# Local attention after a convolution block: P's blocks moved by SP's DMA queue, and another order of the work of images 1 to 3

## The chip, the cores and the metric

The kernel runs on one core of a Trainium2 chip. The metric is the device time of one execution in microseconds, as the median of several runs. Engines are named as in the profile: PE (TensorE, matmul; PEld is its weight load), DVE (VectorE), ACT (ScalarE), POOL (GpSimd), SP (SyncE, which here only issues DMAs).

## The reference, cut to what matters

There are 16 images of 32 x 32 pixels with 128 channels, float32.

```python
perceived = depthwise_conv3x3(x, w_perc) + b_perc        # 128 -> 384 channels
hid = gelu(w_up1 @ perceived + b_up1)                    # 256 channels
h = x + w_up2 @ hid + b_up2                              # 128 channels
q, k, v = split(h @ w_qkv.T + b_qkv)
scores = [(q * shifted(k, dy, dx)).sum(-1) / sqrt(128) for dy, dx in the 3 x 3 window]   # zero padded
w = softmax(scores)                                      # over the 9 positions
out = h + sum_i w[i] * shifted(v, dy_i, dx_i)
```

## The kernel before

Depthwise filters and `w_up1` are folded into one 3 x 3 convolution from 128 to 256 channels. It is computed with a transform along the row (four pixels, six products `M_ORDER`), so that an image needs, for each half of the 256 channels, six **units** of nine products each (L469: three row taps, each as high x high, low x high, high x low, since an operand is split into a rounded "high" part and the "low" rest). Units 0 to 5 are half 0, units 6 to 11 half 1. For every image n the engines do:

- DVE `transform_ab` and `transform` and POOL `differences` and `sums_ab` form the transformed pixels `t`; ACT `high_t` rounds them to `thi`, DVE `low_t` subtracts to `tlo`.
- PE units write PSUM banks. ACT `take_m13` copies one bank, DVE `combine` (ps_sb, ru_sb), `combine_y` (four lines, L1043 to L1049) and `finish_y` (L1057) make `y`. ACT `gelu` (L716) makes `hid`, ACT `high_hid` (L726) rounds it, POOL `low_hid` (L1345) subtracts.
- PE `up(n)` (L524) is the second product, for image n - 1: six products that need the first channel half's high and low parts, four that need the rounding of the second half (`hhi_done`), two that need its low part (`hlo_done`). DVE `sum_h` adds x to give h. ACT `high_h` and DVE `low_h` split h, PE `project_q_parts` (L560 to L563), ACT `take_q`, PE `project_v` (L568) and `score` (L577) follow. A score is a tile of 128 queries against 96 near keys.
- DVE `softmax_front` adds keys for the zero padding and takes the row maxima; ACT takes the exponentials (L795, eight tiles, `exp`); DVE `sums` the reciprocals; POOL `normalise` (L1352); DVE `turn_p` (L1111) transposes P by 32 x 32 blocks into `ptc`.
- The 32-row blocks of `ptc` have to stand at other partitions and columns in `pt`, where PE `values` (L594) reads them. `place_p` on ACT does this with twelve copies (L781, one for each of four rows and three neighbouring rows, 32 partitions x 7 or 8 tiles x 32 numbers). DVE `add_h` adds h to the values, and SP stores the result.

`body(n)` of each engine handles the convolution of image n, the attention scores of image n - 1, the placing of P of image n - 2, and values of image n - 3. Below, numbers in brackets are the arguments in the code, so `up(2)` is in body 2 and multiplies image 1's hid; `gelu(1,1)`, `high_hid(1,1)` and `low_hid(1,1)` are the second half of image 1. "Image n" as a stretch of time is body n. Orders are written out by hand; semaphores count each step. Bodies 0 to 2 have orders of their own, 3, 14 and 15 and the loop in between (bodies 4 to 13) share one. Each engine works strictly in its written order.

The loads and stores are issued by SP in this order: planes of image n + 2, rows of image n + 1 (after `sum_h`), stores. An exponential needs another ACT table than gelu; `prime_gelu` behind the exponentials brings gelu's back.

Of the kernel before, what the change touches and what calls it, by code (L numbers as in the profile page):

```python
# [83 lines left out]
def build(nc, x_planes, x_rows, w_perc, b_perc, w1_c, b_up1, w2_c, b_up2, wqk_c, wv_c, b_qkv, ident_bf_c,  # L84
          mask_c, zero_c, out):
    with ExitStack() as ctx:
# [168 lines left out]
        pt_done = sem("pt_done")  # L255
        pt_dve_done = sem("pt_dve_done")
# [17 lines left out]
        PLACED = TR * 3  # L274
        LATE = ((B - 3, 0), (B - 3, 1), (B - 2, 0), (B - 2, 1), (B - 1, 0))
# [81 lines left out]
        def _(sp):  # L357
# [44 lines left out]

            def body(n, par, conv, attn, store, more):
                if conv and (not isinstance(n, int) or n + 2 < B):

                    sp.wait_ge(ab_done, n * 2 + 2)
                    sp.wait_ge(fcge_done, n * 3 + 3)
                    load_planes(n + 2, par)
                if attn and (not isinstance(n, int) or n + 1 < B):

                    sp.wait_ge(h_done, n * 2)
                    load_rows(n + 1, 1 - par)
                if store and from_image(n, 3):
                    store_out(n)
# [6 lines left out]
        def _(pe):  # L421
# [18 lines left out]
            def small_weights():  # L440
                pe.wait_ge(weights_in, 16 * N_W)
                wq, wk = wqk_in[:, 0, :], wqk_in[:, 1, :]
                pe.matmul(work[:, 2, P:2 * P], wq, wk, start=True, stop=True)
                pe.matmul(work[:, 2, 2 * P:2 * P + 1], wq, bqk[:, 1:2], start=True, stop=True)
                pe.matmul(work[:, 2, 2 * P + 1:2 * P + 2], wk, bqk[:, 0:1], start=True, stop=True)
                pe.wait_ge(biases_in, 48)
                for g in range(2):
                    for m in range(3):
                        last = pe.matmul(work[:, 2, g:g + 1], w1T[:, m, g * P:(g + 1) * P], bp[:, m:m + 1],
                                         start=(m == 0), stop=(m == 2))  # L450
                last.then_inc(b1_ready, 1)
                pe.wait_ge(bq_wide_done, 1)
                pe.matmul(work[:, 2, 2 * P + 2:2 * P + 3], bq_wide[:, :], bqk[:, 1:2], start=True,
                          stop=True).then_inc(wt_ready, 1)
                for _ in range(4):
                    last = pe.matmul(m_ps[:, 2, S:CH], w1T[:, 0, 0:P], w1T[:, 0, 0:S], start=True, stop=True)
                last.then_inc(warm_done, 1)
# [124 lines left out]
            def values(n, hp, g):  # L582

                if not isinstance(n, int) or n < B:

                    pe.wait_ge(v_done, n * 3 - 6)
                    pe.wait_ge(pt_done, n * PLACED - 2 * PLACED)
                    pe.wait_ge(rmax_done, n * 8 + (4 * g - 12))
# [10 lines left out]
            def last_attention():  # L599
# [8 lines left out]
                pe.wait_ge(pt_done, (n - 2) * PLACED)  # L608
# [24 lines left out]
                pe.wait_ge(pt_done, (n - 2) * PLACED + 6)  # L633
# [6 lines left out]
                for g, fillers in enumerate((5, 3)):  # L640
                    for _ in range(fillers):
                        pe.matmul(s_ps[:, 0, 0:S], whi[:, M_ORDER[0], 0, 0:P], thi[:, 0, 0, :], start=True, stop=True)
                    pe.wait_ge(pt_done, (n - 2) * PLACED + 12 + 6 * g)
                    pe.wait_ge(pt_dve_done, 12 + 6 * g)
                    values(n + 2, 1, g)
# [46 lines left out]
        def _(act):  # L692
# [90 lines left out]
            def place_p(n, par, rows):  # L783

                if isinstance(n, int) and n == 2:
                    act.wait_ge(zeroed, 5)
                act.wait_ge(ptc_done, n * 2 - 2)
                if from_image(n, 4):
                    act.wait_ge(o_ready, n * 2 - 6)
                for row in rows:  # L790
                    place(par, row)
# [53 lines left out]
            def body(n, par, conv, attn, store, more):  # L845
# [8 lines left out]
                if is_image(n, 1):  # L854
# [11 lines left out]
                    gelu(1, 1)  # L866
                    for i in range(T):
                        exp(1, i)
                    prime_gelu()
                    return  # L870
                if is_image(n, 2):
                    high_hid(1, 1)
                    take_m13(2, 0)
                    place_p(2, 0, (0, 1, 2))
                    for c in range(NCH):
                        high_h(2, 1, c)
                    place_p(2, 0, (3,))
# [9 lines left out]
                    return  # L887
                if attn:
                    gelu(n - 1, 1)
# [4 lines left out]
                if store:  # L894
                    place_p(n, par, (0, 1, 2, 3))
# [23 lines left out]
        def _(dve):  # L919
# [59 lines left out]
            for k, i in enumerate(TAPS):  # L979

                for m in (1, 2):
# [9 lines left out]
                    if k == 1 and m == 1:  # L991
                        transform_ab(0, 0)
# [109 lines left out]
            def turn_p(n, g):  # L1102

                dve.wait_ge(pn_done, n * 2 + (g - 1))
                if is_last(n):
                    dve.wait_ge(pt_done, (n - 2) * PLACED + 6)
                    dve.wait_ge(pt_dve_done, 6)
                elif from_image(n, 2):
                    dve.wait_ge(pt_done, n * PLACED - PLACED)
# [102 lines left out]
            def body(n, par, conv, attn, store, more):  # L1212
# [12 lines left out]
                if is_image(n, 1):  # L1225
# [12 lines left out]
                    for g in range(2):  # L1238
                        sums(1, g)
                        turn_p(1, g)  # L1240
                    return
                if is_image(n, 2):
                    transform_ab(3, 1)
                    combine(2, 0)
                    sum_h(2, 0)
                    low_h(2, 1)
# [6 lines left out]
                    sums(2, 0)  # L1253
                    combine_y(2, 1)
                    finish_y(2, 1)
                    turn_p(2, 0)
                    sums(2, 1)
                    turn_p(2, 1)
                    return
# [44 lines left out]
        def _(pool):  # L1304
# [67 lines left out]
            def body(n, par, conv, attn, store, more):  # L1372
# [10 lines left out]
                else:  # L1383
# [58 lines left out]
```

## Time and profile before

| what | us |
|---|---|
| median of 3 runs (lowest, highest) | 404.14 (403.94, 404.82) |
| the profiled execution | 405.43 |
| its span, first to last instruction | 403.1 |
| PE busy in the span | 386.1 (96%) |
| DVE busy | 340.5 (84%) |
| ACT busy | 320.6 (80%) |
| POOL busy | 177.4 (44%) |

The busy time of an engine is the union of its instructions; issuing a DMA and waiting are not counted. PE's granted clock is given as a share of full speed (1.00 is 2.4 GHz). "Idle before, releaser" names what ended an engine's gap. A `x2` in the rows in order of time means that neighbouring instructions of one form were merged.

### The profile page before, as it was taken

How to read it: one execution, taken by the hardware profiler on the slowest of the kernel's cores; microseconds unless marked ns; L12 is line 12 of the kernel's file. 1: busy time of each engine (PE TensorE's matmuls, PEld its weight loads, DVE VectorE, ACT ScalarE, POOL GpSimd, SP SyncE). 2: the span in 40 equal slices, each digit the busy share in tenths (PEclk: the TensorE clock that was granted, in tenths of full speed). 3: DMA queues.
4: the chain of work that ended last, by engine and by line, in shares of the span. 5: the costliest groups of instructions: out<-in, count | busy, mean ns of one | idle time of the engine just before them, and what ended most of it. 6: DMA issues, size and time to landing. Idle time of an engine off the chain costs nothing.

```text
span 403.1 us, 10500 instructions
## 1 busy us (share of the span) xinstructions
PE 386.1 (96%) x3674; PEld 362.9 (90%) x3674; DVE 340.5 (84%) x922; ACT 320.6 (80%) x710; POOL 177.4 (44%) x156
## 2 busy tenths in 40 slices
PE   6999975999999999999999999999999999999994
PEld 5999964998999999999999999999999999999874
DVE  5999975798898888888898888889888888886785
ACT  7635568789797997979798897979799797978873
POOL 6785164362626354351636354351636345032110
PEclk9999996999999999999999999999999999999999
DMA  7420300204013050504013050503104030301003
GB/s 232 167 65 2 120 0 18 101 2 146 28 55 116 2 172 1 169 0 131 38 34 135 0 169 0 169 0 104 65 12 157 0 104 2 104 2 54 3 37 120
DMA packets 11513, 28.57 MB, mean 71 GB/s; under 512 B 2400, under 2 KB 3296, under 8 KB 11488
## 3 DMA queue, kind: packets, MB, share of 16 engines
q1 hardware_dynamic: 11200, 28.21, 20.6%
q8 instruction: 14, 0.23, 0.2%
q14 instruction: 11, 0.09, 0.1%
q10 hardware_dynamic: 288, 0.05, 0.1%
HBM read 19.86 MB, written 8.39 MB: 70 GB/s over the span
## 4 chain that ended last, share of the span: by engine, by line
PE 73%; DVE 4%; issue 1%; POOL 0%; DVEq 0%; ACT 0%
PE m_ps L469 39%; PE s_ps L594 8%; PE work L524 8%; PE work L568 6%; PE s_ps L577 5%; PE s_ps L563 2%; PE s_ps L560 1%; PE s_ps L561 1%; PE work L594 1%; DVE t L946 1%; PE work L547 0%; DVE o_sb L1120 0%; PE m_ps L606 0%; DVE ptc L1111 0%; DVE pt L1126 0%
## 5 line engine op out<-in xcount | busy, mean ns | idle before, releaser
L469 PE MATMUL m_ps<-thi,whi 128*128 128x256 f32 x558 | 159.7, 286 | 0.7 <-DVE ru_sb L1034 0.4
L469 PE MATMUL m_ps<-thi,wlo 128*128 128x256 f32 x558 | 156.2, 280 | 0.0
L469 PE MATMUL m_ps<-tlo,whi 128*128 128x256 f32 x558 | 155.0, 278 | 0.0
L469 PEld LDWEIGHTS m_ps<-thi,whi 128*128 128x128 f32 x558 | 105.7, 189 | 4.0 <-issue 1.0
L469 PEld LDWEIGHTS m_ps<-tlo,whi 128*128 128x128 f32 x558 | 106.5, 191 | 0.7
L469 PEld LDWEIGHTS m_ps<-thi,wlo 128*128 128x128 f32 x558 | 105.6, 189 | 0.0
L1345 POOL TENSOR_TENSOR hid_lo<-hid,hid_hi 128x1024 fp32r<-128x1024 f32 x30 | 72.4, 2412 | 24.9 <-ACT hid_hi L726 20.4
L781 ACT COPY pt<-ptc 32x256 f32<-32x256 f32 (+3 forms) x186 | 73.0, 393 | 5.5 <-DVE ptc L1111 1.0
L1322 POOL TENSOR_TENSOR fc<-xp 128x512 f32<-128x512 f32 x16 | 21.6, 1347 | 110.1 <-DVE tlo L953 106.7
L716 ACT ACTIVATE hid<-y,b1eff 128x1024 f32<-128x1024 f32 x31 | 35.6, 1150 | 36.5 <-DVE y L1057 26.7
L795 ACT ACTIVATE p_sb<-p_sb,negmax 128x101 f32<-128x101 f32 x128 | 46.8, 369 | 7.0 <-DVE negmax L1092 7.0
L1352 POOL TENSOR_TENSOR p_sb<-p_sb,rsum 128x384 f32<-128x384 f32 x32 | 27.8, 868 | 42.0 <-DVE rsum L1100 41.9
L594 PE MATMUL s_ps<-pt,v_sb 128*128 128x192 f32 (+2 forms) x260 | 39.0, 305 | 0.0
L594 PEld LDWEIGHTS s_ps<-pt,v_sb 128*128 128x128 f32 x260 | 37.3, 190 | 0.0
L1033 DVE TENSOR_TENSOR ps_sb<-m,m_ps 128x512 f32<-128x512 f32 x32 | 21.7, 678 | 15.2 <-ACT m L706 15.2
L726 ACT CAST hid_hi<-hid 128x1024 fp32r<-128x1024 f32 x30 | 31.5, 1051 | 0.1
L953 DVE TENSOR_TENSOR tlo<-t,thi 128x1024 fp32r<-128x1024 f32 (+1 forms) x30 | 28.1, 978 | 2.7 <-ACT thi L700 2.7
L568 PEld LDWEIGHTS work<-wvT,h_around 128*128 128x128 f32 x240 | 29.1, 192 | 1.2
L700 ACT CAST thi<-t 128x1024 fp32r<-128x1024 f32 (+1 forms) x32 | 25.1, 832 | 5.8 <-DVE t L946 5.6
L568 PE MATMUL work<-wvT,h_around 128*128 128x129 f32 x240 | 29.2, 275 | 0.0
L524 PE MATMUL work<-hid_hi,w2hi 128*128 128x512 f32 x60 | 23.8, 397 | 4.0 <-ACT hid_hi L726 3.7
L1330 POOL TENSOR_TENSOR t<-ab 128x256 f32<-128x256 f32 x16 | 11.8, 738 | 35.8 <-DVE ab L938 35.8
(157 smaller groups left out, 787.5 us busy)
## 6 DMA issues: line engine op xcount, KB each, us to landing
xp<-x_planes SPq DMA_DIRECT2D x16, 640.0 KB, 5.2
xr<-x_rows SPq DMA_DIRECT2D x16, 512.0 KB, 4.0
out<-o_sb SPq DMA_DIRECT2D x28, 256.0 KB, 4.1
out<-y SPq DMA_DIRECT2D x3, 256.0 KB, 2.4
w1T<-w SPq DMA_DIRECT2D x1, 384.0 KB, 3.0
out<-y SPq DMA_DIRECT2D x2, 128.0 KB, 2.5
w2T<-w SPq DMA_DIRECT2D x1, 128.0 KB, 4.4
wqk_in<-w_qk SPq DMA_DIRECT2D x1, 128.0 KB, 4.3
```

The source lines that it names most:

```text
L469: last = pe.matmul(bank[:, col + first:col + end], a[:, j, dy, half * P:(half + 1) * P], c[:, par, T_PLACE[j], first + by:end + by], start ...
L524: return pe.matmul(up_bank(n, c), w[:, half * C:(half + 1) * C], h[:, half, c * CH:(c + 1) * CH], **kw)
L568: last = pe.matmul(v_bank(n, part)[:, u * VT:(u + 1) * VT], h_of(n - 1, hp)[:, W + i * P:W + (i + 1) * P], wvT[:, :], start=True, stop=True)
L594: last = pe.matmul(o_bank(n, g)[:, (first - g * half) * W:(end - g * half) * W], v_of(n - 3, hp)[:, i, :], pt[:, hp, i, (first - above) * ...
L700: nc.scalar.copy(thi[:, par, part, :], t[:, part, :]).then_inc(thi_done, 1)
L716: nc.scalar.activation(hid[:, half, :].rearrange("p (r k s) -> p k r s", k=K4, s=WIN), y[:, half, :, :].rearrange("p k (r s) -> p k r s", ...
L726: nc.scalar.copy(hid_hi[:, half, :], hid[:, half, :]).then_inc(hhi_done, 1)
L781: nc.scalar.copy(pt[to_rows, hp, to_there, to_cols], ptc[rows, there, cols]).then_inc(pt_done, 1)
L795: nc.scalar.activation(p_sb[:, i, 0:KEYS], p_sb[:, i, 0:KEYS], ACT.Exp, bias=negmax[:, i:i + 1], scale=-1.0, accum_out=p_sum[:, i:i + 1]). ...
L953: nc.vector.tensor_tensor(tlo[:, par, part, :], t[:, part, :], thi[:, par, part, :].bitcast(F32), ALU.subtract).then_inc(tlo_done, 1)
L1345: nc.gpsimd.tensor_tensor(hid_lo[:, half, :], hid[:, half, :], hid_hi[:, half, :].bitcast(F32), ALU.subtract).then_inc(hlo_done, 1)
L1352: nc.gpsimd.tensor_tensor(p_sb[:, tiles, 0:NEAR], p_sb[:, tiles, 0:NEAR], rsum[:, tiles].unsqueeze(2).to_broadcast([P, 4, NEAR]), ALU.mult ...
```

## The change

P's blocks are no longer copied by ACT in bodies 2 to 15, but moved by twelve DMA transfers of SP's queue, issued after the planes' load and ahead of the rows' load. They count on a semaphore of their own, `pt_moved` (16 for each transfer, `MOVED` is 192 an image), on which PE's `values` and DVE's `turn_p` now wait. The last image keeps copies on ACT and DVE.

In body 1 ACT rounds the second half of image 1's hid and takes the next bank ahead of the exponentials; POOL forms image 3's differences before the low halves, waits until DVE has made y, does both low halves in a row and only then normalises. DVE's order changes in bodies 1 to 3, and body 3 gets an order of its own on ACT and DVE. In the front, there are three warm-up products instead of four, and `transform_ab(0, 0)` stands one line later.

```diff
@@ SP's program
+            def move_p(n, par):
+                if isinstance(n, int) and n == 2:
+                    sp.wait_ge(zeroed, 5)
+                sp.wait_ge(ptc_done, n * 2 - 2)
+                for row in range(TR):
+                    for rows, there, cols, to_rows, to_there, to_cols in p_blocks(row):
+                        sp.dma_start(pt[to_rows, par, to_there, to_cols], ptc[rows, there, cols]).then_inc(pt_moved, 16)
             def body(n, par, conv, attn, store, more):
                 if conv and (not isinstance(n, int) or n + 2 < B):
                     sp.wait_ge(ab_done, n * 2 + 2)
                     sp.wait_ge(fcge_done, n * 3 + 3)
                     load_planes(n + 2, par)
+                if store:
+                    move_p(n, par)
                 if attn and (not isinstance(n, int) or n + 1 < B):
                     sp.wait_ge(h_done, n * 2)
@@ PE: small_weights, values, last_attention
-                for _ in range(4):
+                for _ in range(3):
                     last = pe.matmul(m_ps[:, 2, S:CH], w1T[:, 0, 0:P], w1T[:, 0, 0:S], start=True, stop=True)
...
-                    pe.wait_ge(pt_done, n * PLACED - 2 * PLACED)
+                    pe.wait_ge(pt_moved, n * MOVED - 2 * MOVED)
...
-                pe.wait_ge(pt_done, (n - 2) * PLACED)
+                pe.wait_ge(pt_moved, (n - 2) * MOVED)
...
-                pe.wait_ge(pt_done, (n - 2) * PLACED + 6)
+                pe.wait_ge(pt_done, 6)
@@ ACT: body
                     gelu(1, 0)
                     high_hid(1, 0)
                     gelu(1, 1)
+                    high_hid(1, 1)
+                    take_m13(2, 0)
                     for i in range(T):
                         exp(1, i)
                     prime_gelu()
                     return
                 if is_image(n, 2):
-                    high_hid(1, 1)
-                    take_m13(2, 0)
-                    place_p(2, 0, (0, 1, 2))
                     for c in range(NCH):
                         high_h(2, 1, c)
-                    place_p(2, 0, (3,))
...
+                if is_image(n, 3):
+                    gelu(2, 1)
+                    high_hid(2, 1)
+                    take_m13(3, 0)
+                    for c in range(NCH):
+                        high_h(3, 0, c)
+                    for c in range(NCH):
+                        take_q(3, c)
+                    high_t(4, 0)
+                    gelu(3, 0)
+                    take_m13(3, 1)
+                    high_hid(3, 0)
+                    for i in range(T):
+                        exp(3, i)
+                    prime_gelu()
+                    return
...
-                if store:
-                    place_p(n, par, (0, 1, 2, 3))
@@ DVE: first taps, turn_p, body
-                    if k == 1 and m == 1:
-                        transform_ab(0, 0)
+                        if k == 1 and m == 2 and dy == 0:
+                            transform_ab(0, 0)
...
-                    dve.wait_ge(pt_done, n * PLACED - PLACED)
+                    dve.wait_ge(pt_moved, n * MOVED - MOVED)
...
                     softmax_front(1, 1)
-                    for g in range(2):
-                        sums(1, g)
-                        turn_p(1, g)
+                    transform_ab(3, 1)
+                    sums(1, 0)
+                    combine(2, 0)
+                    turn_p(1, 0)
+                    sums(1, 1)
                     return
                 if is_image(n, 2):
-                    transform_ab(3, 1)
-                    combine(2, 0)
                     sum_h(2, 0)
+                    turn_p(1, 1)
                     low_h(2, 1)
...
                     combine(2, 1)
-                    sums(2, 0)
                     combine_y(2, 1)
                     finish_y(2, 1)
+                    sums(2, 0)
                     turn_p(2, 0)
                     sums(2, 1)
                     turn_p(2, 1)
+                    return
+                if is_image(n, 3):
+                    transform_ab(4, 0)
+                    combine(3, 0)
+                    for g in range(2):
+                        add_h(3, 0, g)
+                    sum_h(3, 1)
+                    low_h(3, 0)
+                    transform(4, 0)
+                    combine_y(3, 0)
+                    finish_y(3, 0)
+                    low_t(4, 0)
+                    softmax_front(3, 1)
+                    sums(3, 0)
+                    combine(3, 1)
+                    turn_p(3, 0)
+                    sums(3, 1)
+                    combine_y(3, 1)
+                    turn_p(3, 1)
+                    finish_y(3, 1)
                     return
@@ POOL: body
                 if is_image(n, 1):
                     low_hid(0, 1)
                     sums_ab(2)
-                else:
+                    differences(3, 1)
+                    pool.wait_ge(y_part_done, 16)
+                    low_hid(1, 0)
+                    low_hid(1, 1)
+                    normalise(1, 0)
+                    sums_ab(3)
+                    normalise(1, 1)
+                    return
+                if not is_image(n, 2):
                     if more:
                         sums_ab(n + 1)
```

## Rows read from the trace of the kernel before

**Rows 1.** Windows: busy time (instructions) by engine, granted clock, DMA share.

```profile
50.00:60.00 10.00, 8.25 (x60) 7.31 (x60) 8.14 (x31) 6.51 (x20) 6.57 (x5) 1.00 0.00 0
60.00:70.00 10.00, 4.88 (x19) 4.17 (x20) 5.55 (x12) 8.38 (x17) 4.55 (x4) 0.70 0.04 5
64.00:66.00 2.00, 0.00 (x0) 0.00 (x0) 0.21 (x1) 1.88 (x6) 2.00 (x1) 0.51 0.00 0
200.00:250.00 50.00, 50.00 (x486) 47.98 (x486) 42.73 (x117) 43.32 (x93) 24.14 (x21) 1.00 0.20 68
```

**Rows 2.** Chain that ended last, in the loop: start, length.

```profile
131.44 2.83 PE s_ps L594 x20
...
154.32 2.83 PE s_ps L594 x20
```

**Rows 3.** PE's waits, whole execution: total, times, longest.

```profile
PE work L524 <- ACT hid_hi L726: 3.7, 1, 3.7
PE work L524 <- POOL hid_lo L1345: 2.7, 1, 2.7
```

**Rows 4.** PE in order of time: start, length, operation.

```profile
49.89 0.39 PE L469 MATMUL m_ps<-thi,whi 128*128 128x256 f32 x1
...
57.11 0.47 PE L524 MATMUL work<-hid_hi,w2hi 128*128 128x512 f32 x1 [0.25 <-DVE v_sb L1065]
...
62.46 0.50 PE L524 MATMUL work<-hid_hi,w2hi 128*128 128x512 f32 x1 [3.73 <-ACT hid_hi L726]
...
66.31 1.22 PE L524 MATMUL work<-hid_lo,w2hi 128*128 128x512 f32 x2 [2.66 <-POOL hid_lo L1345]
...
104.22 0.28 PE L469 MATMUL m_ps<-thi,whi 128*128 128x256 f32 x1
```

**Rows 5.** ACT in order of time.

```profile
54.48 1.15 ACT L716 ACTIVATE hid<-y,b1eff 128x1024 f32<-128x1024 f32 x1 [3.44 <-DVE y L1057]
...
61.38 1.03 ACT L726 CAST hid_hi<-hid 128x1024 fp32r<-128x1024 f32 x1
...
62.92 3.79 ACT L781 COPY pt<-ptc 32x224 f32<-32x224 f32 x9
...
111.14 5.06 ACT L781 COPY pt<-ptc 32x224 f32<-32x224 f32 x12
```

**Rows 6.** Page, costliest groups: out<-in xcount, busy, mean ns, idle before.

```profile
L795 ACT ACTIVATE p_sb<-p_sb,negmax 128x101 f32<-128x101 f32 x128 | 46.8, 369 | 7.0 <-DVE negmax L1092 7.0
```

**Rows 7.** POOL in order of time.

```profile
38.21 2.40 POOL L1345 TENSOR_TENSOR hid_lo<-hid,hid_hi 128x1024 fp32r<-128x1024 f32 x1 [0.50 <-ACT hid_hi L726]
...
50.31 1.47 POOL L1322 TENSOR_TENSOR fc<-xp 128x512 f32<-128x512 f32 x1 [6.91 <-DVE tlo L953]
...
63.91 2.35 POOL L1345 TENSOR_TENSOR hid_lo<-hid,hid_hi 128x1024 fp32r<-128x1024 f32 x1
```

**Rows 8.** DVE in order of time, images 0 and 1.

```profile
38.25 2.64 DVE L1047 SCALAR_TENSOR_TENSOR y<-ru_sb 128x256 f32<-128x256 f32 x1
...
50.49 1.58 DVE L1044 SCALAR_TENSOR_TENSOR y<-ps_sb 128x256 f32<-128x256 f32 x1
```

**Rows 9.** DVE in order of time, turn_p of image 3.

```profile
104.87 0.58 DVE L1111 STREAM_TRANSPOSE ptc<-p_sb 128x384 f32<-128x384 f32 x1 [0.16 <-POOL p_sb L1352]
...
107.38 0.57 DVE L1111 STREAM_TRANSPOSE ptc<-p_sb 128x384 f32<-128x384 f32 x1
```

**Rows 10.** SP's DMA issues in order of time.

```profile
1.19 0.42 SPq L362 DMA_DIRECT2D xp<-x_planes  x1
...
6.47 0.43 SPq L362 DMA_DIRECT2D xp<-x_planes  x1
...
117.73 0.35 SPq L366 DMA_DIRECT2D xr<-x_rows  x1
```

**Rows 11.** DMA, 6 to 7 us: packets, MB, share; KB each, us to landing.

```profile
q1 hardware_dynamic: 758, 0.12, 74.9%
...
zeros<-zero_keys SPq DMA_DIRECT2D x1, 20.0 KB, 2.4
```

More of the change, by code:

```diff
@@ L255, in build @@
         pt_done = sem("pt_done")
+        pt_moved = sem("pt_moved")
         pt_dve_done = sem("pt_dve_done")
@@ L274, in build @@
         PLACED = TR * 3
+        MOVED = PLACED * 16
         LATE = ((B - 3, 0), (B - 3, 1), (B - 2, 0), (B - 2, 1), (B - 1, 0))
@@ L642, in last_attention @@
                         pe.matmul(s_ps[:, 0, 0:S], whi[:, M_ORDER[0], 0, 0:P], thi[:, 0, 0, :], start=True, stop=True)
-                    pe.wait_ge(pt_done, (n - 2) * PLACED + 12 + 6 * g)
+                    pe.wait_ge(pt_done, 12 + 6 * g)
                     pe.wait_ge(pt_dve_done, 12 + 6 * g)
@@ L783, in place_p @@
             def place_p(n, par, rows):
-                if isinstance(n, int) and n == 2:
-                    act.wait_ge(zeroed, 5)
                 act.wait_ge(ptc_done, n * 2 - 2)
-                if from_image(n, 4):
-                    act.wait_ge(o_ready, n * 2 - 6)
+                act.wait_ge(o_ready, n * 2 - 6)
                 for row in rows:
@@ L1105, in turn_p @@
                 if is_last(n):
-                    dve.wait_ge(pt_done, (n - 2) * PLACED + 6)
+                    dve.wait_ge(pt_done, 6)
                     dve.wait_ge(pt_dve_done, 6)
                 elif from_image(n, 2):
-                    dve.wait_ge(pt_done, n * PLACED - PLACED)
+                    dve.wait_ge(pt_moved, n * MOVED - MOVED)
                 tiles = slice(4 * g, 4 * g + 4)
```

## The prediction

> **What bounds the kernel now.** I read the windows first, then PE's waits, then the order of time on each engine. In the loop PE is busy without a gap at full granted clock (200 to 250 us stands for all its stretches) [rows 1], and one image follows the next at 22.88 us (values of image 5 at 131.44, of image 6 at 154.32) [rows 2]. The reader is to see that nothing taken off ACT, DVE or SP there can shorten the loop: it can only keep PE fed or fail to. PE's gaps lie ahead of 100 us: in 50 to 70 us it is busy 13.13 of 20 us, and from 64 to 66 us, and on in the units behind, its granted clock is 0.51 (1.2 GHz instead of 2.4), after two gaps in which it waited for a rounding on ACT (3.7 us) and a low half on POOL (2.7 us) [rows 1, 3, 4].
>
> How much is there to win? PE begins image 2 at 49.89 and image 4 at 104.22 [rows 4], 54.33 us. A loop image is 22.88 us, and image 2 has no values (2.83 us [rows 2]), so 20.05. 20.05 + 22.88 = 42.93, and **11.4 us** are lost. They are: about 1.0 up to the start of up(2) at 57.11, ahead of unit 4 and of up(2) itself; the gap to 62.46 after six products (3.9) and the gap to 66.31 after four more (2.9); and 3.6 for the rest, which is the low clock of the last two products and of units 6 to 8, and small waits in image 3 [rows 3, 4].
>
> **Images 1 to 3.** Why the two gaps? gelu(1,1) runs at 54.48, but the eight exponentials of image 1 with their table load stand before high_hid(1,1), which comes at 61.38; low_hid(1,1) on POOL comes behind normalise and sums_ab, 63.91 to 66.26 [rows 5, 7]. The change puts both ahead. Walking the queues with the measured durations:
>
> POOL's differences(3,1) waits for transform(2,0) alone and starts at about 46.6 instead of 50.31, so most of it is gone when combine_y(1,1) comes at 50.15; there it held up DVE (1.58 us for a line that takes 0.4 where nothing holds it) [rows 7, 8]. It now meets low_t(2,0) instead. I take 0.7 to 1 us of that as left: combine_y done at 52.45 in place of 53.8, finish_y at 53.05 in place of 54.4. Bounds: 52.2 with no collision, 54.4 if all of it comes back. gelu(1,1) then ends at 54.2 and high_hid(1,1) at 55.25; low_hid(1,0) runs from 52.5 to 54.9, low_hid(1,1) from 55.3 to 57.7 (2.4 each [rows 7]). A unit takes PE 1.04 us and a product of up 0.23, so PE reaches up(2) at 49.89 + 6 x 1.04 = 56.13 and needs that last half ten products on, at 58.45: both gaps are covered, by 0.75 us. up(2) ends at 58.9, not 67.3, and PE is never idle long enough to repeat what came before the drop to 0.51 (gaps of 3.9 and 2.9 us).
>
> On these DVE stretches the rows show whole instructions held: an L1047 of some 0.4 us took 2.64 from 38.25 on, to the end of a POOL subtraction of 2.40 us from 38.21 [rows 7, 8]. The Trainium skill (SBUF — State Buffer, "Who interferes with whom") says of this that a VectorE instruction with two SBUF inputs and a GpSimd one that reads SBUF exclude each other for the whole instruction. The trace agrees, 2.64 against 0.4 us; by that rule every coincidence of the new order costs up to a whole instruction.
>
> What is late next? The exponentials: high_hid and take_m13 (1.6 us) now stand in front, against 1.4 won by the earlier gelu, so they end about where they did: 53.1 + gelu 1.1 + 1.05 + 0.6 + the table's 1.3 + 8 x 0.37 = 60.05 [rows 5, 6]. transform_ab(3,1) waits behind low_hid(1,1) to 57.7; sums(1,0) has to wait for the exponentials to 58.7 anyway. Then DVE runs as one chain: combine 1.2, turn_p and sums 0.6, sum_h(2,0) from 60.6 (1.4), turn_p(1,1) at 62.0 behind normalise, low_h 1.3, transform 1.4, combine_y 1.35, finish_y 0.6, low_t 1.8, softmax_front 3.3, combine(2,1) 1.2, to 73.5 (a 256-column line counts 0.34 and a 512-column one 0.6 to 0.7, as DVE's lines follow one another in the loop, where turn_p's takes 0.57 [rows 9]). PE passes it so: units 6 to 8 to 58.9 + 3 x 1.04 = 62.05; the query products wait for h_hi (ACT is free of table loads at 61.65) and h_lo, **0.75 lost**; so image 3 begins at 70.65 (query products 1.4, v 1.8, scores 1.5, units 9 to 11 3.1), its units 0 and 1 end at 72.75, and unit 2 waits for ru_sb until 73.5, **0.75 lost**. values(3) at 75.6. In image 3 turn_p(2,1) ends at about 79.2, sums_ab(4) and low_hid(2,1) follow to 83.8, where PE wants the latter at 82.8: **1.2 lost** with the restart. Query products then don't wait. Image 4 begins at about 95.3, its unit 2 waits for ru_sb once more, **0.6 lost**. After that DVE has slack per image (busy 42.7 of 50 us [rows 1]) and PE closes up.
> Sum: 11.4 - (0.75 + 0.75 + 1.2 + 0.6) = **8.1 us gained**. Bounds: 11.4 if none of the four waits appears, about 4 if DVE is held some more.
>
> **P's blocks by DMA.** Off ACT come 12 copies per image, 5.06 us from 111.14 on [rows 5]. ACT isn't what PE waits for in the loop, so that is worth nothing there; in image 2 it takes 3.79 us from in front of high_h, which the walk above has used. On SP twelve issues are added: at the start SP issues one every 0.47 us (1.19 to 6.47 in eleven steps, 0.48) whatever the shape [rows 10]; 12 x 0.48 = 5.8 us. The trace has no transfer within SBUF and none of 32 partitions by 7 or 8 runs of 128 bytes. Packets: 94 blocks of 32 rows make 3008 per image. In 6 to 7 us, 758 packets of mostly under 512 B went in 1 us at a share of 74.9%, that is 16 ns each on an engine [rows 11]; 3008 x 16 / 16 = 3 us, hidden under the issues. A 20 KB load of 128 runs landed 2.4 us after issue [rows 11]. So the moves end 5.8 + 2.4 = 8.2 us after turn_p. Range of one transfer: 0.35 us (a rows load's issue) up to the whole 2.4 one after the other.
> Who waits? turn_p(n,1) ends at 107.38 + 0.57 = 107.95 and the next turn_p(n+1,0), which overwrites ptc, is due 104.87 + 22.88 = 127.75: 19.8 us of room, 8.2 used [rows 9]. PE's values(5) at 131.4 has more. In image 2: turn_p(1,1) ends 62.6, moves land by about 71, turn_p(2,0) is due at 76 and values(3) at 75.6. Behind the moves on SP: the rows' load, issued at 117.73 in the loop and wanted some 21 us later; stores, with as much; the planes' load stands ahead of them [rows 10]. SP has to be free at 117.7, and is at 113.8. All this is costed at nothing; the cover is 11.6 us of turn_p's room.
>
> The row shows issues 0.47 apart while landings take 2.4 us, so they overlap. The Trainium skill (DMA: Bandwidth & Descriptors, "Rules for kernel authors") speaks against the change: many small transfers are to be made one, since under 64 KB one pays mostly overhead; these have 28 to 32 KB. Taken as time in series that overhead would be the first rival below; taken as latency, it changes nothing here.
>
> **The front.** One warm-up product less frees PE 0.4 us at 16.0, but wlo of L969 ends at 16.24 and DVE is busy without a break to 22.5, the last lows arriving just in time (PE's m_ps row from 16.43 on is not held up, yet has no more than 0.1 to gain). transform_ab(0,0), one line later, avoids a held line (0.78 for 0.41), and then meets POOL's sums_ab. Taken as 0; bounds -0.2 to +0.4 us of gain. Tail: the same work in the same order, 0.
>
> **How this stands to the median.** The profiled execution took 405.43 us, 2.33 around its span of 403.1; 405.43 - 8.1 = 397.3. It lies 1.3 above the median of 404.14, so the forecast is 404.14 - 8.1 = **396.0 us**.
>
> **Rivals.**
> 1. *The moves are in series.* Each transfer holds the queue until it has landed. The loop closes over turn_p(n,1) -> twelve transfers -> turn_p(n+1,0) -> turn_p(n+1,1). With 3.1 us between the two turn_p and 2.4 landing, the period is 12x + 5.5, which reaches 22.88 at x = 1.45 us per transfer. The gain is eaten over some 13 images from x = 1.5. At 2.4 us, 34.3 per image, 11.4 x 13 = 148 us more: 544. At 1.6 us, 24.7, 1.8 x 13 = 24 more: **420 us**. For it: no such transfer in the trace. Against it: fourteen issues in a row at 0.47. 5%.
> 2. *DVE takes ACT's place.* finish_y(1,1) stays at 54.4 (1.35 later), and one further line of the DVE chain is held by a low half, 2.4: gain 8.1 - 3.8 = 4.3, **399.8 us**. For it: DVE has no gap in the new image 2, and POOL works beside it nearly throughout, as in the held line of [rows 7, 8]. 16%.
> 3. *Nothing late comes next.* The four small waits vanish: 404.14 - 11.4 = **392.7 us**. Against: chains that arrive within a us of PE. 12%.
> 4. *It does nothing:* gaps of the same size reappear at up(2), as each image's values wait for P elsewhere. **404.1 us**. Against: both roundings depend on nothing that ends after 55 us. 4%.
> The forecast: 63%, on its own between 393.5 and 398.5.
>
> A difference of 0.2%, 0.8 us, is about what can be told from none. Faster: 63 + 16 + 12 and a little of the fourth's 4, 92%. Same 3%. Slower 5%. The range reaches from rival 3 to rival 2: 392.5 to 399.8; outside lie the first and fourth and the tails, some 18%.
>
> **What the new profile would show.** PE's wait for hid_hi gone and that for hid_lo under 1.5 us; granted clock 1.00 through 60 to 70; the exponentials of image 1 still near 57 to 60; small waits of PE for ru_sb and h_lo; values 22.88 apart from image 4 on; pt's copies on ACT only in the last image; twelve SP issues of pt 0.4 to 0.5 us apart, landing in about 2.4. Wrong if DVE's ptc (L1111 of before) waits for a DMA, or the loop's period is not 22.88, or low_hid(1,1) starts after 56.

## The result, and the profile after

The changed kernel takes **397.32 us** (median of 4, 397.25 to 397.45); the kernel before, in the runs beside it, 404.45 (403.94 to 404.82). The ratio of the means is 0.9825, 95% interval 0.9808 to 0.9842: 7.1 us faster. Two executions below in which the chip's clock was low throughout, 546.72 us in run 1 and 436.73 us of the kernel before beside runs 9 to 12, are left out of medians and ratios. The forecast was 396.0 us in a range of 392.5 to 399.8. The profiled executions lie further apart than the medians: 405.43 and 397.33 us, spans 403.1 and 395.2, so 7.9 in the span, where the walk had claimed 8.1.

Windows of the changed kernel (busy time and instructions of PE, PEld, DVE, ACT, POOL; granted clock; DMA share; GB/s), to be laid beside [rows 1]:

```profile
50.00:60.00 10.00, 10.00 (x76) 9.51 (x76) 9.64 (x35) 8.02 (x22) 6.37 (x5) 1.00 0.00 0
60.00:70.00 10.00, 9.79 (x128) 8.86 (x127) 9.91 (x25) 8.47 (x12) 3.11 (x5) 1.00 0.20 31
96.00:119.00 23.00, 22.04 (x214) 20.27 (x213) 19.62 (x54) 15.23 (x33) 11.24 (x10) 1.00 0.34 93
200.00:250.00 50.00, 50.00 (x486) 47.77 (x485) 43.66 (x117) 32.98 (x67) 21.23 (x18) 1.00 0.33 89
```

Where PE was busy 13.13 of 20 us between 50 and 70, it is now busy 19.79, and its granted clock stays at 1.00. In the loop PE still has no gap (200 to 250 us). ACT's busy time there went from 43.32 to 32.98 of 50 us and changed nothing; the DMA share went from 0.20 to 0.33. Behind image 3, PE still has gaps in 96 to 119 us: that is image 4.

PE's waits (total, times, longest), against [rows 3]:

```profile
PE m_ps L483 <- DVE ru_sb L1057: 1.1, 3, 0.4
...
PE work L538 <- POOL hid_lo L1389: 0.7, 1, 0.7
PE s_ps L577 <- DVE h_lo L986: 0.5, 2, 0.3
PE s_ps L574 <- ACT h_hi L815: 0.2, 1, 0.2
```

The wait of 3.7 us for hid_hi is gone, the 2.7 us for hid_lo are 0.7. Seven small ones are what is left, one of them in image 1 as before; PE's order of time places the others (image 2 begins at 49.78 and image 4 at 94.95; 99.75 and 123.76 are values of images 4 and 5), against [rows 4]:

```profile
49.78 0.39 PE L483 MATMUL m_ps<-thi,whi 128*128 128x256 f32 x1
...
56.12 0.40 PE L538 MATMUL work<-hid_hi,w2hi 128*128 128x512 f32 x1
...
58.42 0.62 PE L538 MATMUL work<-hid_lo,w2hi 128*128 128x512 f32 x2
...
62.96 0.50 PE L577 MATMUL s_ps<-h_lo,wqk_hi 128*128 128x512 f32 x1 [0.21 <-DVE h_lo L986]
...
73.07 0.38 PE L483 MATMUL m_ps<-thi,whi 128*128 128x256 f32 x1 [0.27 <-DVE ru_sb L1057]
...
83.31 0.74 PE L538 MATMUL work<-hid_lo,w2hi 128*128 128x512 f32 x2 [0.70 <-POOL hid_lo L1389]
...
94.95 0.28 PE L483 MATMUL m_ps<-thi,whi 128*128 128x256 f32 x1
...
97.57 0.38 PE L483 MATMUL m_ps<-thi,whi 128*128 128x256 f32 x1 [0.38 <-DVE ru_sb L1057]
...
99.75 0.44 PE L608 MATMUL s_ps<-pt,v_sb 128*128 128x160 f32 x2
...
110.96 0.47 PE L574 MATMUL s_ps<-h_hi,wqk_hi 128*128 128x512 f32 x1 [0.25 <-ACT h_hi L815]
...
112.00 0.50 PE L577 MATMUL s_ps<-h_lo,wqk_hi 128*128 128x512 f32 x1 [0.34 <-DVE h_lo L986]
...
123.76 0.44 PE L608 MATMUL s_ps<-pt,v_sb 128*128 128x160 f32 x2
```

ACT, the rounding now at 54.01 and not 61.38, against [rows 5]:

```profile
52.83 1.15 ACT L730 ACTIVATE hid<-y,b1eff 128x1024 f32<-128x1024 f32 x1 [1.90 <-DVE y L1080]
54.01 1.05 ACT L740 CAST hid_hi<-hid 128x1024 fp32r<-128x1024 f32 x1
...
55.56 1.28 ACT L806 ACT_TABLE_LOAD   x1
```

POOL, low_hid(1,1) now at 55.14 and not 63.91, low_hid(2,1) at 80.86 and low_hid(3,0) at 94.84, against [rows 7]:

```profile
46.58 1.33 POOL L1366 TENSOR_TENSOR fc<-xp 128x512 f32<-128x512 f32 x1 [3.27 <-DVE t L969]
...
52.22 2.42 POOL L1389 TENSOR_TENSOR hid_lo<-hid,hid_hi 128x1024 fp32r<-128x1024 f32 x1 [1.97 <-DVE y L1072]
55.14 2.41 POOL L1389 TENSOR_TENSOR hid_lo<-hid,hid_hi 128x1024 fp32r<-128x1024 f32 x1 [0.50 <-ACT hid_hi L740]
...
80.86 2.39 POOL L1389 TENSOR_TENSOR hid_lo<-hid,hid_hi 128x1024 fp32r<-128x1024 f32 x1
...
94.84 2.40 POOL L1389 TENSOR_TENSOR hid_lo<-hid,hid_hi 128x1024 fp32r<-128x1024 f32 x1
```

DVE, against [rows 8]: low_t(2,0) (its two lines take 2.50), a line of combine_y(1,1) free of POOL (0.41, not 1.58), sum_h(2,0), and turn_p(3,0), which comes late for image 4 (see below):

```profile
48.30 2.50 DVE L976 TENSOR_TENSOR tlo<-t,thi 128x1024 fp32r<-128x1024 f32 x2 [0.67 <-ACT thi L714]
...
51.06 0.41 DVE L1067 SCALAR_TENSOR_TENSOR y<-ps_sb 128x256 f32<-128x256 f32 x1
...
60.32 1.38 DVE L1223 SCALAR_TENSOR_TENSOR h_around<-work,b,xr 128x512 f32<-128x512 f32 x2
...
98.06 0.58 DVE L1134 STREAM_TRANSPOSE ptc<-p_sb 128x384 f32<-128x384 f32 x1 [0.54 <-POOL p_sb L1396]
```

SP's issues, against [rows 10], and beneath the moves' own line, L413 (duration of an issue and landing, least, median and most):

```profile
62.40 8.50 SPq L413 DMA_DIRECT2D pt<-ptc  x12
```

```profile
L413 SPq DMA_DIRECT2D pt<-ptc x168: 592/611/1761, 62.4 to 359.1; - x168
...
DMA to landing us min/median/max: 1.9/1.9/3.6
```

Twelve issues take 8.50 us here, 0.71 each with what lies between them, and 7.8 us, 0.65 each, in most of the loop; a transfer lands 1.9 us after its issue in the median. No instruction of DVE or PE waits for them.

### The profile page after: what moved, and what is told of

Read it like the earlier page. It is cut to its first block, busy times and chain, and to the rows that moved or that the text cites. A ratio compares the mean times of both kernels' runs of the same rounds, so it can differ in the third digit from the quotient of the medians.

```text
span 395.2 us, 10483 instructions
## 1 busy us (share of the span) xinstructions
PE 383.7 (97%) x3672; PEld 360.5 (91%) x3672; DVE 337.5 (85%) x922; ACT 256.3 (65%) x542; POOL 178.1 (45%) x156
## 3 DMA queue, kind: packets, MB, share of 16 engines
q1 hardware_dynamic: 56000, 33.61, 30.3%
## 4 chain that ended last, share of the span: by engine, by line
PE 72%; DVE 15%; issue 5%; POOL 4%; ACT 2%; DMA 1%; DVEq 0%; ACTq 0%; POOLq 0%
PE m_ps L483 38%; PE work L538 8%; PE s_ps L608 8%; PE work L582 6%; PE s_ps L591 5%; DVE t L969 2%; PE s_ps L577 2%; PE s_ps L574 1%; PE s_ps L575 1%; DVE tlo L976 1%; POOL hid_lo L1389 1%; POOL p_sb L1396 1%; DVE y L1066 1%; DMA wp<-w_perc 1%; DVE y L1080 1%
## 5 line engine op out<-in xcount | busy, mean ns | idle before, releaser
L815 ACT CAST h_hi<-h_around 128x512 fp32r<-128x512 f32 x30 | 18.2, 620 | 22.6 <-DVE h_around L1223 22.4
L976 DVE TENSOR_TENSOR tlo<-t,thi 128x1024 fp32r<-128x1024 f32 (+1 forms) x30 | 28.7, 997 | 0.9 <-ACT thi L714 0.9
L822 ACT ACTIVATE q_sb<-s_ps,bq_s 128x512 f32<-128x512 f32 x30 | 20.6, 688 | 12.3 <-PE s_ps L577 12.3
L1088 DVE TENSOR_TENSOR v_sb<-work,bv 128x384 f32<-128x384 f32 (+1 forms) x45 | 23.0, 512 | 6.3 <-PE work L582 5.2
```

What stands on the lines that cost most here:

```text
L976: nc.vector.tensor_tensor(tlo[:, par, part, :], t[:, part, :], thi[:, par, part, :].bitcast(F32), ALU.subtract).then_inc(tlo_done, 1)
L1088: nc.vector.tensor_tensor(v_of(n - 1, hp)[:, first:end, :], sums[:, :, 0:C], bv[:, :].unsqueeze(1).to_broadcast([P, len(tiles), C]), ALU.a ...
```

## The experiments

Each was timed beside the kernel before on its chip; the first four shared one chip, the next four one, the last four one. The kernel before stood at medians of 405.54, 405.22 and 405.03 us there.

**1. The order alone.** P's blocks copied by ACT again.

```diff
-                if store:
-                    move_p(n, par)
...
                     high_hid(2, 0)
+                    place_p(2, 0, (0, 1, 2, 3))
...
                     take_m13(3, 0)
+                    place_p(3, 1, (0, 1, 2, 3))
...
                     high_hid(n - 1, 1)
+                if store:
+                    place_p(n, par, (0, 1, 2, 3))
```

> The changed kernel with its orders, but P's blocks copied by ACT again (in image 2 behind high_hid(2,0), in image 3 behind take_m13(3,0), then as before). If the whole gain is the order and the moves are worth nothing to PE, it is as the changed kernel, 397.3 us. My theory: the order wins both large gaps by itself, but ACT is busy from 61 to 75 us in the changed kernel, so 5.06 us of copies there put the exponentials of image 2, then gelu(2,1) and low_hid(2,1) off by as much; PE has about 1 us of room: some 3.5 us lost again, 400.8 us (399 to 402). The loop stays at 22.88 us per image, since ACT is busy under 90% of it.

401.19 us (400.82 to 402.05), ratio 0.9901 (0.9871 to 0.9930). PE's waits, and ACT in order of time (copies of image 2, the table for its exponentials, high_hid(2,1)):

```profile
PE work L536 <- POOL hid_lo L1394: 1.5, 1, 1.5
...
PE s_ps L572 <- ACT h_hi L816: 1.0, 1, 1.0
PE work L536 <- ACT hid_hi L738: 0.8, 1, 0.8
```

```profile
69.50 5.07 ACT L793 COPY pt<-ptc 32x224 f32<-32x224 f32 x12
74.59 1.28 ACT L807 ACT_TABLE_LOAD   x1
...
81.49 1.05 ACT L738 CAST hid_hi<-hid 128x1024 fp32r<-128x1024 f32 x1
```

The copies push the table load from 69.46 to 74.59 and high_hid(2,1) to 81.49, where PE waits for it (0.8), then for its low part (1.5). In image 4 the copies end at 112.78, and high_t and h_hi come behind them, where PE waits again (1.0). So the order alone is worth about 4 us, and some 4 come only together with the moves. In the loop values follow at 22.88 with the copies on ACT (150.57, 173.46). No run takes the new order of ACT and that of DVE apart.

**2. The moves alone.** The kernel before, with `move_p` on SP and all `place_p` of bodies 2 to 15 taken off ACT, waits renumbered as in the change.

```diff
+                if store:
+                    move_p(n, par)
...
-                    place_p(2, 0, (0, 1, 2))
...
-                    place_p(2, 0, (3,))
...
-                if store:
-                    place_p(n, par, (0, 1, 2, 3))
```

> The kernel before with the twelve transfers per image in place of ACT's copies, and nothing else. My theory: PE's two gaps come from the order of image 1 alone, so they stay (3.7 and 2.7 us) and the time is that of before, 404.4 us, within 0.5. Rival: ACT's 5 us are what image 2 and 3 lack, then 2 us or more are gained, 402.4 or less. Second rival: the moves hurt, over 405.2.

404.46 us beside 405.54, ratio 0.9973 (0.9958 to 0.9989): 1.1 us faster, a little more than expected. PE's wait for hid_hi is 3.7 us as before, that for hid_lo 1.8 instead of 2.7:

```profile
66.16 1.22 PE L536 MATMUL work<-hid_lo,w2hi 128*128 128x512 f32 x2 [1.78 <-POOL hid_lo L1350]
```

But this is no gain: the last products come at 66.16, where they came at 66.31, and the wait is shorter because the four products ahead of it already ran at the low clock (0.42 to 0.59 us apart and not 0.23 to 0.34; granted clock 0.50 in 62 to 64 us, where the kernel before has 1.00). The values of image 5 stand at 131.48, against 131.44. So in the rows of PE the moves alone change nothing, as the theory had it. Where the 1.1 us of the medians come from is not shown; the spans of the executions overlap (401.5 to 403.0, against 402.0 to 404.1).

**3. The front of before** in the changed kernel.

```diff
-                for _ in range(3):
+                for _ in range(4):
                     last = pe.matmul(m_ps[:, 2, S:CH], w1T[:, 0, 0:P], w1T[:, 0, 0:S], start=True, stop=True)
...
+                    if k == 1 and m == 1:
+                        transform_ab(0, 0)
-                        if k == 1 and m == 2 and dy == 0:
-                            transform_ab(0, 0)
```

> The changed kernel with the front of before (four warm-up products, transform_ab(0,0) after the second group of taps). I costed the front's edits at 0, bounds -0.2 to +0.4: 397.3 us expected, 397.7 at most if they are worth their bound.

396.78 us, ratio 0.9796 (0.9767 to 0.9824), against 397.32 (0.9825) and 397.07 (0.9808) for the changed kernel on two other chips. The intervals overlap: the front's edits are worth nothing that can be told. PE begins image 2 at 49.59 here, and at 49.78 and 49.96 in the two profiles of the changed kernel.

**4. The gaps filled.** The kernel before, PE kept busy through its two gaps.

```diff
+                def fill(count):
+                    if is_image(n, 2):
+                        pe.wait_ge(rmax_done, 8)
+                        for _ in range(count):
+                            pe.matmul(s_ps[:, 0, 0:S], whi[:, M_ORDER[0], 0, 0:P], thi[:, 0, 0, :], start=True, stop=True)
+                fill(30)
                 pe.wait_ge(hhi_done, n * 2)
...
+                fill(22)
                 pe.wait_ge(hlo_done, n * 2)
```

> The kernel before with idle-time products in PE's two gaps of up(2): 30 of 256 columns in the first, 22 in the second (they write a bank that the next query products overwrite). They leave both waits as they are. If the low granted clock after the gaps costs what the rows show (units 6 to 8 in 4.75 instead of 3.13 us, the last two products in 0.9 instead of 0.5), the time falls by 1.6 to 2.1 us, to 402.5. If the low clock cost nothing by itself, because DVE is late there anyway, it stays at 404.4.

402.69 us, ratio 0.9934 (0.9909 to 0.9960), 2.9 by the medians of that chip. The window, and PE at the last two products of up(2) and at the first query product:

```profile
60.00:70.00 10.00, 9.75 (x75) 9.08 (x74) 5.77 (x13) 8.60 (x18) 4.62 (x4) 1.00 0.06 16
```

```profile
66.23 0.72 PE L524 MATMUL work<-hid_lo,w2hi 128*128 128x512 f32 x2
...
69.91 0.40 PE L568 MATMUL s_ps<-h_hi,wqk_hi 128*128 128x512 f32 x1
```

The last products still come at 66.23 (66.31 before), so both waits end where they did; but the clock stays at 1.00, two products take 0.72 and not 1.22 us, and the query products start at 69.91, not at 72.08. 2.2 us of what those gaps cost was the slow clock behind them (1.2 GHz), which this kernel gets back with no change of order.

**5 and 6. Smaller moves.** Each transfer split by tiles in two and in three.

```diff
-        MOVED = PLACED * 16
+        MOVED = PLACED * 32      # 48 with three parts
...
-                for row in range(TR):
-                    for rows, there, cols, to_rows, to_there, to_cols in p_blocks(row):
+                for row, tiles in [(r, t) for r in range(TR) for t in (range(0, 4), range(4, 8))]:
+                    for rows, there, cols, to_rows, to_there, to_cols in p_blocks(row, tiles):
```

> The changed kernel with each of the twelve transfers split in two by tiles: 24 per image, 16 KB each. In the changed kernel twelve issues take 8.6 to 9.0 us in the loop, 0.72 each, and the last lands 1.9 us later. The loop closes over the moves at 24x + 1.9 + 3.1: at x = 0.72 22.3 us, just under PE's 22.88, so the time stays at 397.3 us (to 399, where an image at the start is caught). If transfers were in series with their landings (2.6 each), the changed kernel itself would not hold 22.88, and this one would need 67 us per image.

> Split in three: 36 per image, 8 to 12 KB each. If one issue costs 0.72 us whatever its size, the period is 36 x 0.72 + 5.0 = 30.9 us, 8.0 more than PE's, over 12 to 13 images some 100 us: 495 us, and DVE's transpose into ptc waits for a DMA. If an issue's price goes with its blocks (0.72 us for 8, so 0.25 to 0.3 for 3), nothing is lost: 397 to 400. A fixed part of 0.48, as at the kernel's start, gives 22.3 and some microseconds lost: 397 to 405.

With 24 transfers: 404.19 us, ratio 0.9969 (0.9952 to 0.9986). PE's values(3), DVE's turn_p(2,0), the window behind, and SP's issues in the loop:

```profile
80.79 5.89 PE L608 MATMUL s_ps<-pt,v_sb 128*128 128x160 f32 x20 [5.46 <-issue]
```

```profile
80.80 0.58 DVE L1134 STREAM_TRANSPOSE ptc<-p_sb 128x384 f32<-128x384 f32 x1 [5.22 <-DMA pt<-ptc]
```

```profile
80.00:84.00 4.00, 3.21 (x13) 3.24 (x13) 2.26 (x6) 0.00 (x0) 1.15 (x2) 0.54 0.84 260
```

```profile
108.87 16.11 SPq L413 DMA_DIRECT2D pt<-ptc  x24
```

24 issues take 16.11 us, 0.67 each. In the loop this is hidden and the period is 22.88. But image 2 of the changed kernel gives the moves only from 62.3 to 75.3, where values(3) needs them. Here the 24 issues last to 79.5. PE's values(3) and turn_p(2,0), which both have a wait for `pt_moved`, start together at 80.8. PE names no releaser for its 5.46 us ("issue"), but this wait on the moves is the one in its code. After it the granted clock is 0.54, and the twenty products take 5.89 and not 2.99 us. The wait and the 2.9 us of slow clock make 8.4; the 0.70 us wait for hid_lo in up(3) goes, and the span is 7.7 us longer. I had looked at the loop's room alone, and expected 397.3.

With 36: 476.39 us, ratio 1.176 (1.173 to 1.179). turn_p(n,0) of three images in a row, and SP's issues:

```profile
116.42 0.58 DVE L1134 STREAM_TRANSPOSE ptc<-p_sb 128x384 f32<-128x384 f32 x1 [3.73 <-DMA pt<-ptc]
...
144.85 0.58 DVE L1134 STREAM_TRANSPOSE ptc<-p_sb 128x384 f32<-128x384 f32 x1 [5.99 <-DMA pt<-ptc]
...
173.53 0.58 DVE L1134 STREAM_TRANSPOSE ptc<-p_sb 128x384 f32<-128x384 f32 x1 [6.62 <-DMA pt<-ptc]
```

```profile
119.52 24.21 SPq L413 DMA_DIRECT2D pt<-ptc  x36
```

An issue costs 0.67 us for 3 blocks (0.64 in most of the loop), hardly less than for 8 (0.71, and 0.65), so its price goes by transfers, not by bytes or runs. That is the first of the three cases, but at 0.67 and not 0.72, so 476 and not 495 us. The transposes lie 28.43 and 28.68 apart; 36 x 0.67 + 1.8 + 3.1 = 29.0 (with the later issues of 0.64, images follow at 27.3). The chain that ended last is SP's issues for 63% of the span.

**7 and 8. The small waits.** combine(3,1) ahead of sums(3,0) on DVE, and then also low_hid(2,1) ahead of sums_ab(4) on POOL.

```diff
-                    sums(3, 0)
-                    combine(3, 1)
+                    combine(3, 1)
+                    sums(3, 0)
...
+                if is_image(n, 3):
+                    low_hid(2, 1)
+                    sums_ab(4)
```

> The changed kernel with DVE's combine(3,1) ahead of sums(3,0), which waits 0.75 us for an exponential while PE's unit 2 of image 4 waits for ru_sb (0.38 plus restart). My theory: that wait goes, and DVE's chain, which PE meets again at the query products of image 4 (waits of 0.25 and 0.34), moves ahead by up to 0.75: 0.6 to 1.2 us gained, 396.4. Rival: DVE's chain in image 4 is released by y of image 3, which PE's own units give, then only 0.1 to 0.5: 397.0.

397.24 us, ratio 0.9809 (0.9788 to 0.9830): no gain that can be told.

> As the run with combine first, and in image 3 POOL's low_hid(2,1) ahead of sums_ab(4). The 0.70 us wait of PE's up(3) for hid_lo goes, since the rounding ends at 77.87 and the low half now ends at about 80.6 instead of 83.25; transform_ab(4,0) on DVE is held until then, 1.7 us that DVE has idle before sum_h (2.18). Expected another 0.3 to 0.9 us: 395.9. Rival: the held line moves the whole of DVE's chain, and PE meets it at image 4: no gain over the run with combine first.

396.62 us, ratio 0.9797 (0.9775 to 0.9820), 0.6 us under run 7 beside it, though not at 395.9. The spans of the five executions of each don't overlap (394.5 to 394.9, against 395.2 to 395.7), so this gain is real. PE in image 4 of the run with combine first (run 7):

```profile
107.05 0.50 PE L538 MATMUL work<-hid_lo,w2hi 128*128 128x512 f32 x1 [0.34 <-POOL hid_lo L1389]
...
111.17 0.47 PE L574 MATMUL s_ps<-h_hi,wqk_hi 128*128 128x512 f32 x1 [0.26 <-ACT h_hi L815]
...
112.20 0.50 PE L577 MATMUL s_ps<-h_lo,wqk_hi 128*128 128x512 f32 x1 [0.34 <-DVE h_lo L986]
```

There the wait of unit 2 for ru_sb is gone. A new one stands at 107.05 for hid_lo, and the two ahead of the query products are as long as they were (0.26, 0.34): the chain of image 4 is not released by combine(3,1). The wait that was moved came back 10 us later. The profile shows what does release it. In the changed kernel turn_p(3,0) waits for POOL's normalise(3,0), which runs straight behind low_hid(3,0) (94.84 to 97.24); in this run low_hid(3,0) stands at 95.06 and turn_p(3,0) at 98.27, 0.2 us later, just as sum_h(2,0) already was (60.54 against 60.32). combine(3,1) has no part in it.

**9. The changed kernel again**, as a base for the last three.

> The changed kernel itself, beside the next three on one chip, so that differences of half a microsecond can be read: 397.3 us.

397.07 us (396.98 to 398.12), ratio 0.9808 (0.9784 to 0.9832).

**10. Without POOL's wait for y.**

```diff
                     differences(3, 1)
-                    pool.wait_ge(y_part_done, 16)
                     low_hid(1, 0)
```

> The changed kernel without POOL's wait for image 1's y (no data depends on it). POOL is then free at 50.25 and takes low_hid(1,0) at 50.92, in the middle of combine_y(1,1), whose four lines take 50.72 to 52.14. My theory, whole instructions held: the later lines stand until about 53.4, finish_y and gelu(1,1) come 2.3 us later, low_hid(1,1) ends at about 59.9 instead of 57.55, PE waits some 1.5 us in up(2) and the chain of DVE another: 1.5 to 2.3 us slower, 399.2. Rival: the two share what they read and only slow each other a little: 397.3 to 397.8.

399.26 us, ratio 0.9856 (0.9834 to 0.9878), 2.2 over the changed kernel beside it. DVE's second line of combine_y(1,1), POOL's low_hid(1,0), and two of PE's waits:

```profile
51.18 2.62 DVE L1067 SCALAR_TENSOR_TENSOR y<-ps_sb 128x256 f32<-128x256 f32 x1
```

```profile
51.12 2.40 POOL L1389 TENSOR_TENSOR hid_lo<-hid,hid_hi 128x1024 fp32r<-128x1024 f32 x1 [0.74 <-ACT hid_hi L740]
```

```profile
55.22 0.36 PE L483 MATMUL m_ps<-thi,whi 128*128 128x256 f32 x1 [0.89 <-DVE y L1080]
...
64.36 0.47 PE L574 MATMUL s_ps<-h_hi,wqk_hi 128*128 128x512 f32 x1 [0.47 <-ACT h_hi L815]
```

A line of 0.41 us takes 2.62 and ends 0.3 after POOL's. PE pays ahead of unit 4 (0.89, for y), not in up(2) as I had written, and again at the query products (0.47 and 0.22). A wait that no data needs is worth 2.2 us.

**11. differences(3,1) late.**

```diff
+                    pool.wait_ge(tlo_done, 6)
                     differences(3, 1)
```

> The changed kernel, with POOL's differences(3,1) waiting for tlo of image 2 as before (it starts near 50.1 and not 46.58) and so meeting combine_y(1,1) instead of low_t(2,0). By my step y is then finished near 54.4 instead of 52.75, low_hid(1,1) ends near 59.3, PE waits about 1 us in up(2) and meets the later chain of DVE: 1 to 2 us slower, 398.9. Rival: what the collision costs is covered by the room of 0.75 us and more: 397.3.

398.59 us, ratio 0.9838 (0.9816 to 0.9859), 1.5 over the changed kernel. combine_y's lines take 1.58, 0.90 and 0.98 us again, as in the kernel before. y is finished at 54.46 and low_hid(1,1) ends at 59.25, as the step had it; but PE pays in four small waits, 0.23 ahead of unit 4, 0.26 ahead of up(2), and 0.49 and 0.22 at the query products, not inside up(2).

**12. Both reorders with the old front.**

> The best version: combine(3,1) ahead of sums(3,0), low_hid(2,1) ahead of sums_ab(4), with the front of before, whose run came out 0.5 us under the changed kernel on another chip. If the fronts are worth the same, 396.6 us as with the new front; if the old one is the better, 396.1.

396.69 us (396.18 to 397.86), ratio 0.9797 (0.9770 to 0.9823). With run 8 it has the lowest median. That is 0.4 us under the changed kernel beside it, which the spread of the times covers; the spans are apart (394.3 to 394.7, against 395.2 to 395.4), so the two reorders are worth some 0.8 us in the span.

## Why the prediction was right

*PE bounds the loop, and relief of ACT there is worth nothing.* Right: 22.88 us per image in the changed kernel, with ACT's copies (run 1) and without.

*11.4 us are lost between 49.89 and 104.22.* The same stretch, start of image 2 to start of image 4, now takes 94.95 - 49.78 = 45.17 us instead of 54.33: 9.2 gained. The walk had 8.7 up to there. So the waits up to there were priced 0.5 us too high. The walk's single times: up(2) without a gap from 56.12 (56.13 was forecast), sum_h(2,0) at 60.32 (60.6), low_hid(1,1) ending at 57.55 (57.7), the exponentials in their old place, unit 2 of image 3 at 73.07 (73.5), up(3)'s last products at 83.31 (83.8).

*Four small waits.* Three stand where they were put, each smaller: query products of image 2 0.21 with its restart for 0.75, ru_sb 0.27 for 0.75, hid_lo 0.70 for 1.2. These are the idle times alone; a restart adds 0.2 to 0.3 (the first product behind a gap comes a little after its release and takes 0.38 to 0.50 us instead of 0.28 to 0.40). The fourth, unit 2 of image 4, cost 0.6 as forecast (values(4) follow the image's start by 4.80 and not 4.17 us).

*After that PE closes up.* This is the step that was mis-sized. Image 4 loses again: values(5) follow values(4) by 24.01 us, where the kernel before has 22.88 (108.39 to 131.27), so 1.1 us, at h_hi (0.25), h_lo (0.34) and their restarts. DVE's slack, 7.3 us of 50 in the window I took it from and so 3.3 per image, is not a reserve at this place. The chain that ended last runs from low_hid(2,1) at 80.86 over up(3), sum_h, low_h and low_t to POOL's differences at 92.16 and low_hid(3,0) at 94.84, then over normalise, turn_p(3,0), finish_y, gelu and take_m13 to h_lo at 111.26, for which PE waits. DVE and POOL hold it in turn, and from there on it comes 22.46 us later per image (sum_h at 109.35 and 131.81), 0.4 less than PE's 22.88, so that from image 5 on PE no longer waits. 9.2 + 0.1 (start of image 2) - 0.6 - 1.1 = 7.5, and 0.4 more at the last store's issue, 7.9 in the span.

*The span against the median.* 8.1 was the walk and is the difference of the profiled executions (405.43 - 397.33); the medians give 7.1. The forecast subtracted a gain from one execution's rows from a median that the next four runs did not quite repeat (404.14, then 404.45). The profiled execution lay 1.3 us above its median, and the changed kernel's, 397.33, lies on its own median of 397.32: that distance is the whole 1.3 us between 396.0 and 397.3. The kernel before varies more from execution to execution than the changed one. Beside run 1, its 17 spans are 402.0 to 402.9 where the mean granted clock was 0.989 or 0.990, and 403.2 to 404.1 where it was 0.986 or 0.987; the changed kernel's are 395.2 to 395.4. Two profiles show a difference of this kind: the kernel before (0.990) has the low clock only behind its second gap, run 2 (0.987) behind the first already, which is as long, 3.7 us. That this is what parts the 17 spans is likely, but not shown. That the walk itself comes within 0.2 us of the span is partly luck: 1.1 us lost in image 4 are offset by 0.5 from waits put too high, 0.4 at the last store and 0.1 at the start of image 2.

*POOL and DVE hold each other for whole instructions.* Right, and worth what the step said. It is shown by runs 10 and 11: 2.62 us for a line of 0.41, 2.2 and 1.5 us of time. The Trainium skill's rule (SBUF — State Buffer, "Who interferes with whom": VectorE with two SBUF inputs against a GpSimd instruction that reads SBUF, held throughout) agrees with these rows. The collision with low_t was put at 0.7 to 1 us; it cost 0.7 (2.50 for 1.82 us).

*The moves are hidden.* Right, but with an issue of 0.71 in place of 0.48 us: 8.5 + 1.9 = 10.4 us, not 8.2 (7.8 + 1.9 = 9.7 in most of the loop). The difference cost nothing in the changed kernel and would have in one with smaller room; the price per transfer hardly falls with its size (runs 5 and 6). The first rival's mechanism was wrong in one part, since landings overlap (1.9 us each at issues 0.7 apart), but its loop over turn_p is real: it decided at 36 transfers, with 29.0 us computed and 28.4 to 28.7 measured. At 24 it is values(3) in image 2 that decides. The advice against many small transfers (the Trainium skill, DMA: Bandwidth & Descriptors, "Rules for kernel authors") bears on this kernel only from the point where the issues fill the room: 24 transfers cost 7 us, in image 2, and 36 cost 79.

*ACT's copies and the order are two edits.* I costed the moves at nothing but for 3.79 us in front of high_h. In fact about half the gain needs both: the order alone gave 4 us, the moves alone 1 in the medians and nothing in PE's rows, together 7 to 8. In the changed kernel ACT is busy 12.44 of the 14 us from 61 to 75; the walk did not follow ACT beyond 61.65, and so did not say that the order needs the moves.

*The clock.* The 11.4 us contained the slow clock as a remainder. Run 4 shows its size: 2.2 us in the rows of PE (query products at 69.91, not 72.08), with both waits left in. Run 5 shows it once more, from the other side: a gap of 5.46 us in PE was followed by the low clock (0.54 in 80 to 84 us), which cost 2.9 us besides.

## What to carry to other kernels

Where one engine is full in the loop, look for its gaps at the start and walk every engine's queue through them with measured durations, line by line: here that gave the places of four waits within 0.5 us, and missed the two of image 4 (1.1 us). Follow it until two images in a row show no wait, not to the first window in which the other engines look idle. When copies are given to DMA queues, count the transfers and not the bytes, and compare issues plus landing with the shortest room that any image gives, which is here in image 2 and not in the loop; and count every instruction that waits for them, PE's values as well as DVE's transpose. A wait without a data dependence can be worth its line, where POOL and DVE both read SBUF.

## What the hardware showed that I had not expected

An issue of a transfer within SBUF on SP takes 0.64 to 0.72 us from start to start, for 32 x 8, 32 x 4 or 32 x 3 runs of 128 bytes alike, where loads at the kernel's start take 0.48; why is not shown. SP's queue moved 44,800 more packets than before (56,000 against 11,200), which raised the queue's share of the 16 engines from 20.6% to 30.3%, over spans of 403.1 and 395.2 us; that is an estimate of some 13 ns of one engine for each packet.
